# Shared turns with spread routing steps, norms and turned rows written in place, two shared products behind the last expert tile

## The chip, the cores and the metric

The kernel runs on one core of a Trainium2 chip. The metric is the device time of one execution in microseconds; lower is better. The engines of a core are PE (matmul, with its weight loads as PEld), DVE (vector), ACT (scalar, activation tables), POOL (GpSimd) and SP (issues most DMAs). Each has its own queue and takes its instructions in order; they wait for each other by semaphores.

## What is computed

Four residual blocks on `x` of 32 sequences of 256 tokens with 128 columns. The change lies in the first two, retention and a mixture of experts with one expert per token and a shared product:

```python
x = x + _L0_attn_ref(_layernorm(x, axis=-1), ...)
x = x + _L0_ffn_ref(_layernorm(x, axis=-1), ...)

def _L0_ffn_ref(hidden_states, w_router, gate_up_proj, down_proj, w_gate, w_up, w_down):
    x = hidden_states.reshape(-1, h)
    logits = x @ w_router.T
    _, top_idx = jax.lax.top_k(logits, TOP_K)
    mask = jax.nn.one_hot(top_idx, E, dtype=logits.dtype).sum(axis=1)
    scores = jax.nn.sigmoid(logits) * mask
    masked_inputs = scores.T[:, :, None] * x[None, :, :]
    gate_up = jnp.einsum('eth,ehf->etf', masked_inputs, gate_up_proj)
    gate, up = jnp.split(gate_up, 2, axis=-1)
    expert_out = jnp.einsum('etf,efh->eth', up * jax.nn.silu(gate), down_proj)
    shared = jax.nn.silu(x @ w_gate.T) * (x @ w_up.T) @ w_down.T
    out = shared + expert_out.sum(axis=0)
    return out.reshape(b, s, h)
```

Then come an attention over each sequence (the chip time from 423 us on) and a last block on selected rows. They are the same in both kernels.

## The kernel before

`retention_and_experts` is the first program block, up to about 423 us. It has four stages, and each engine's code is written out by hand in the order in which the engine runs it.

**The retention loop.** `pipeline(engine, steps, n, first)` writes, for each turn `it`, the steps in the order of its list; a step with lag k works on sequence `it - k`. The 32 sequences take turns 0 to 31, and the later lags drain in the turns after. For a sequence, DVE takes statistics of the rows (`stats2_of`, `moments2`), POOL turns them into a factor and a shift in four small operations (`inv_std2`), ACT writes the norm (`norm2`, into `h2`, two buffers), PE turns it (`transpose_h2`), ACT copies the turned rows from PSUM (`copy_h2T`, into `h2T`, two buffers), and POOL copies both into buffers for all sequences (`keep_h2` into `h2_all`, `keep_h2T` into `h2T_all`). Every fourth sequence PE multiplies by the router (`route`) and turns the logits (`turn_logits`).

**Shared products and routing.** For each sequence PE does `up(s)` (8 PE instructions in the profile) and `down(s)` (8), ACT the Silu (`gate_of`), DVE the product (`gated`) and the addition to `x` (`add_shared`). `up(s)` waits for the gate and the product of sequence s-2, whose buffers it uses. Beside that DVE finds the expert of each token in two halves of 32 tiles: `choose` (five operations), `span` (a scan), `slots` (row numbers), then `count_tiles` and `find_experts` (four operations of 0.8 us for each half). PE's `count_rows(half)` counts tokens; ACT's `copy_counts` and `score_rows` copy the counts and take the sigmoid. ACT has two activation tables to load for this, Sigmoid and Silu. DVE's `scale_rows(s)` multiplies a sequence's rows by their score, and POOL's `scatter(t)` sends a tile of rows, by an indirect DMA, to their place in DRAM (`sorted_in`): 64 of them. A scatter waits for its rows (`scaled`) and its row numbers (`slot_done`).

**Expert tiles.** SP waits for `expert_done`, for the padding rows and for all 64 scatters, and loads tiles of sorted rows. PE turns them (L1041), multiplies them by their expert's weights (L1050, L1063), 40 pairs of tiles; POOL scatters the results (L517, `y_rows`).

**The end of the block.** SP waits for the last result to be stored (`stored`), starts two loads of results, and all engines meet (L102 to L104) before the attention starts.

In the code before, the shared products begin with `shared_first` at lag 8, one turn for each of the first five; ACT loads the Silu table in `counts_first`; and all operations of `span`, `slots` and `gated` come on DVE after the whole pipeline.

## Time and profile before

| | us |
|---|---|
| median of 3 runs | 1022.21 (1020.53 to 1022.84) |
| profiled execution, device time | 1023.18 |
| its span in the profile | 1021.4 |
| PE busy over the span | 913.6 (89%) |
| DVE, ACT, POOL busy | 716.1, 638.3, 609.7 |
| retention loop, about | 20 to 181 |
| shared products and routing, about | 181 to 290 |
| expert tiles, about | 291 to 411 |
| end of the block, about | 411 to 423 |

The span is the time from the first to the last recorded instruction; the device time has 1.8 us more around it. A busy share is an average over stages with different limits, so the stages are read one by one. In the timelines a row is a run of instructions of one line: its start, its length, engine and line, what is written and read, how many, and in brackets how long the engine sat idle before and who ended it. `banks` is PSUM; `r_v_pad` holds the shared product, `r_qT` the gate, since these buffers are used again; `r_h` is also the small buffer `h2`, and `h` the large one.

### The profile page before, as it was taken

What the parts mean: (1) busy time and instruction counts of PE and PEld (TensorE: products, weight loads), DVE (VectorE), ACT (ScalarE), POOL (GpSimd) and SP (SyncE); (2) the same over time, 40 slices, a digit from 0 to 9 for tenths busy, and PEclk for the clock granted to TensorE, in tenths of its full rate; (3) what the DMA queues carried; (4) which work ended last, traced back from release to release, by engine and by line L of the source; (5) the groups of instructions that cost most, each with busy time, mean ns of one, the idle gap of its engine ahead of it and who ended that gap; (6) DMA issues with size and microseconds to landing.
All of it is one profiled execution on the core that took longest, in us unless ns stands there. A gap on an engine that the chain in (4) does not pass through costs nothing. (4 is left out here: it accounts for less than half of the span.)

```text
span 1021.4 us, 28611 instructions
## 1 busy us (share of the span) xinstructions
PE 913.6 (89%) x10122; PEld 687.7 (67%) x10122; DVE 716.1 (70%) x1564; ACT 638.3 (62%) x1306; POOL 609.7 (60%) x1278
## 2 busy tenths in 40 slices
PE   6999999788989999269999999999999999935776
PEld 5888888677989999145666666666666666524654
DVE  4888898567545444366888888888888888727652
ACT  4777776331224444227888888888888888743552
POOL 4777776566737767554666676766666665334003
PEclk9999999899999999559999999999999999976989
DMA  8200000412123332153353434453444434102000
GB/s 321 116 3 2 3 2 2 135 40 86 51 67 96 96 93 74 56 165 117 118 158 117 140 121 153 132 159 117 137 124 128 137 117 131 42 21 64 4 2 21
DMA packets 68571, 93.71 MB, mean 92 GB/s; under 512 B 11474, under 2 KB 60242, under 8 KB 63954
## 3 DMA queue, kind: packets, MB, share of 16 engines
q1 hardware_dynamic: 63186, 80.76, 25.6%
q0 software_dynamic: 5248, 11.15, 3.1%
q8 instruction: 83, 1.36, 0.6%
q14 instruction: 54, 0.44, 0.1%
HBM read 57.60 MB, written 33.23 MB: 89 GB/s over the span
## 5 line engine op out<-in xcount | busy, mean ns | idle before, releaser
L1461 DVE TENSOR_REDUCE a_neg_max<-a_slot 128x4 f32<-128x1024 f32 x256 | 306.0, 1218 | 79.3 <-PE a_slot L1598 62.1
L1550 ACT ACTIVATE a_pT<-a_slot 128x1024 f32<-128x1024 f32 x256 | 255.5, 1026 | 8.6 <-PE a_slot L1598 5.1
L1631 PE MATMUL a_ps_o<-a_pT,a_v_pad 128*32 128x256 f32 x2048 | 137.9, 387 | 0.0
L1598 PE MATMUL a_slot<-a_k_stack,a_q_stack 62*128 62x256 f32 x1024 | 120.9, 317 | 5.7 <-DMA a_q_stack<-q_dram 3.8
L1598 PE MATMUL a_slot<-a_q_stack,a_k_stack 64*128 64x256 f32 x1024 | 114.6, 312 | 3.6 <-ACT a_pT L1550 1.9
L1598 PEld LDWEIGHTS a_slot<-a_k_stack,a_q_stack 62*128 62x128 f32 x1024 | 79.7, 192 | 48.1 <-issue 22.2
L517 POOL DMA_INDIRECT y_rows<-h,m_token x80 | 81.1, 1014 | 47.0 <-issue 33.0
L1598 PEld LDWEIGHTS a_slot<-a_q_stack,a_k_stack 64*128 64x128 f32 x1024 | 75.5, 187 | 34.8 <-issue 23.4
L560 DVE TENSOR_TENSOR r_score<-banks,r_decay 128x512 f32<-128x512 f32 x128 | 81.3, 677 | 7.0 <-PE banks L917 7.0
L1631 PEld LDWEIGHTS a_ps_o<-a_pT,a_v_pad 128*32 128x32 f32 x2048 | 53.6, 109 | 45.7 <-issue 19.4
L500 POOL DMA_INDIRECT sorted_in<-h,m_slot x64 | 65.3, 1020 | 30.0 <-issue 17.0
L1050 PE MATMUL banks<-r_kT,h 128*128 128x128 f32 x640 | 79.5, 278 | 0.0
L1050 PEld LDWEIGHTS banks<-r_kT,h 128*128 128x128 f32 x640 | 76.1, 195 | 0.0
L745 DVE COPY h<-expert_up 128x512 f32 x80 | 31.3, 433 | 57.4 <-PE banks L1050 56.6
L986 PE MATMUL banks<-h2T,shared_up 128*128 128x256 f32 x256 | 64.6, 399 | 4.3 <-DVE r_v_pad L675 4.3
L758 ACT ACTIVATE r_h<-x,r_shift,r_rstd 128x128 f32<-128x128 f32 x128 | 56.7, 497 | 9.2 <-POOL r_shift L445 8.8
L832 ACT ACTIVATE r_qT<-banks 128x512 f32<-128x512 f32 x32 | 19.1, 597 | 66.3 <-PE banks L986 66.3
L869 ACT ACTIVATE h<-banks 128x512 f32<-128x512 f32 x40 | 23.9, 599 | 57.3 <-PE banks L1050 57.3
L986 PEld LDWEIGHTS banks<-h2T,shared_up 128*128 128x128 f32 x256 | 49.4, 202 | 11.8 <-issue 4.9
L1362 POOL TENSOR_TENSOR a_max_part<-a_neg_max,a_zeros 128x16 fp32r<-128x16 f32 x64 | 13.6, 212 | 71.9 <-DVE a_neg_max L1461 69.6
L1391 POOL TENSOR_TENSOR a_v_pad<-a_v_tok,a_zeros 128x128 f32<-128x128 f32 x64 | 24.2, 399 | 52.4 <-PE a_ps_o L1631 52.4
L1364 POOL TENSOR_TENSOR a_part<-a_qk,a_part 128x256 fp32r<-128x256 f32 x64 | 46.5, 727 | 5.0
(291 smaller groups left out, 2038.0 us busy)
## 6 DMA issues: line engine op xcount, KB each, us to landing
a_k_stack<-k_dram SPq DMA_DIRECT2D x64, 256.0 KB, 3.0
a_q_stack<-q_dram SPq DMA_DIRECT2D x64, 256.0 KB, 3.6
k_dram<-a_part SPq DMA_DIRECT2D x64, 128.0 KB, 2.3
q_dram<-a_part SPq DMA_DIRECT2D x32, 256.0 KB, 2.1
h<-sorted_in SPq DMA_DIRECT2D x80, 66.0 KB, 2.0
expert_up<-in_eu_dram SPq DMA_DIRECT2D x1, 4096.0 KB, 22.7
out_dram<-e_x_plus_h SPq DMA_DIRECT2D x32, 128.0 KB, 2.1
h<-y_rows SPq DMA_DIRECT2D x7, 512.0 KB, 4.3
```

The source lines that it names most:

```text
L500: nc.gpsimd.indirect_dma_start(sorted_in, bass.IndirectOffsetOnAxis(ap=slot[:, t:t + 1], axis=0), h2_all[:, t, :], None).then_inc(scattere ...
L517: nc.gpsimd.indirect_dma_start(y_rows, bass.IndirectOffsetOnAxis(ap=token[:, at:at + 1], axis=0), ye[:, t % RING, j], None).then_inc(store ...
L560: nc.vector.tensor_tensor(score[:, p, tile], ps_score[tile][:], own, ALU.mult).then_inc(score_done, 1)
L745: ins = nc.vector.tensor_copy(w_pair[:, p % 2, j], w_up[:, dve_experts[t][j]])
L758: ins = nc.scalar.activation(h[:, p, t], x_sb[:, s * TPS + t, :], ACT.Identity, bias=shift[:, p, t:t + 1], scale=rstd[:, p, t:t + 1])
L986: ins = nc.tensor.matmul(bank[2 * which + s % 2][:, f * S:(f + 1) * S], shared_up[:, which, f], h2T_all[:, s * S:(s + 1) * S], start=True, ...
L1050: ins = nc.tensor.matmul(bank[PAIR * (p % 2) + j][:, f * P:(f + 1) * P], w_pair[:, p % 2, j, f * P:(f + 1) * P], xeT[:, p % 2, j], start=T ...
L1364: nc.gpsimd.tensor_tensor(low.bitcast(F32R), value, high, ALU.subtract).then_inc(steps, 1)
L1461: nc.vector.tensor_reduce(neg_max[:, p, half, t, :, g], slots[SLOT_OF["m", j]][:].rearrange("p (c r) s -> p c r s", c=TILES), AX.X, ALU.ma ...
L1550: nc.scalar.activation(pT[:, j % PT_RING], slots[SLOT_OF["e", j]][:], ACT.Exp).then_inc(e_read, 1)
L1598: ins = nc.tensor.matmul(slot[:, tile * UT + r], weights[at, n, half, g * UT + r, of_weights].bitcast(F32R), moving[at, n, half, g * UT + ...
L1631: ins = nc.tensor.matmul(ps_o[q * APAD:(q + 1) * APAD, g // 2], v_pad[:, p, t, g * UNIT + q], pT[:, (2 * g + t) % PT_RING, q], start=g % 2 ...
```

## The change

Four things are changed.

1. **Norms and turned rows.** `norm2` writes straight into `h2_all`, `copy_h2T` straight into `h2T_all`. POOL's two copies per sequence are gone, with the waits on them; `scale_rows` now waits for the norm and for its turning.
2. **The drain of the loop.** The first count and `up(0)` stand at lag 3 of the last sequence, `up(1)`, `down(0)`, `up(2)` in the turn after it, and then one `down` and one `up` in each turn. ACT loads the Silu table two turns earlier (`silu_first`). DVE scales the first four sequences inside the loop (`scale_first`) and does the first scan and row numbers ahead of the last sequence's `residual` (`place_first`). POOL sends two tiles ahead of the last `inv_std2`.
3. **Routing of the second half.** DVE's operations of `choose(1, ...)`, `span`, `slots` and `find_experts` are spread over the shared turns 7 to 26, at most one small group for each turn. `LATE_CHOICE` is 7; PE's second count stands in turn 13.
4. **Two sequences later.** With `DEFERRED = 2` the shared products of sequences 30 and 31 come behind the last expert tile, on PE, ACT and DVE.

The core of the diff (renamed parameters, removed semaphores and repeated forms left out):

```diff
-SLOT_STARTS = (0, 8, PART_TILES, PART_TILES + 8)
+SLOT_STARTS = (0, 8, PART_TILES, PART_TILES + 8, PART_TILES + 20)
-LATE_CHOICE = 6
-DRAIN_ROWS = 3
-DRAIN_GATES = 4
-DRAIN_SHARED = 5
+LATE_CHOICE = 7
+DEFERRED = 2
+DRAIN_ROWS = 5
+DRAIN_GATES = 6
+DRAIN_SHARED = 6
...
-            pipeline(pool, [(keep_h2, 6), (inv_std2, 5), (decay_q, 3), (inv_std1, 0), (prepare, 0), (scatter_first, 5), (keep_h2T, 5)],
-                     B, B)
+            pipeline(pool, [(scatter_first(range(0, 2)), 5), (inv_std2, 5), (scatter_first(range(2, DRAIN_ROWS)), 6), 
+                            (decay_q, 3), (inv_std1, 0), (prepare, 0)], B, B)
...
             def scale_rows(s):
-                after(dve, h2_kept, s + 1)
+                after(dve, h2_done, s + 1)
+                after(dve, h2T_done, s + 1)
...
+            def scale_first(s, p, r):
+                if CHOOSE + 5 <= s < CHOOSE + 5 + FIRST_SCALED // 2:
+                    n = 2 * (s - CHOOSE - 5)
+                    if n == 0:
+                        dve.wait_ge(row_score_done, 1)
+                    scale_rows(n)
+                    scale_rows(n + 1)
+
+            def place_first(s, p, r):
+                if s == B - 1:
+                    span(0)
+                    slots(0)
...
+            pipeline(dve, [(stats1_of, 0), (settle2, 5), (decayed_k, 3), (moments2, 5), D_[0], D_[1], (settle1, 0), D_[2],
+                           (mask_state, 3), (moments1, 0), D_[3], (place_first, 4), (residual, 4), (stats2_of, 4), (choose_first, 0),
+                           (scale_first, 0), (gate_first, 4)], B, B)
...
-            for s in range(2, B):
+            for s in range(2, B - DEFERRED):
                 gated(s)
                 add_shared(s - 2)
...
+                if s in range(LATE_CHOICE, LATE_CHOICE + 5):
+                    choose(1, s - LATE_CHOICE)
+                elif s == LATE_CHOICE + 6:
                     span(1)
...
+                elif s in range(LATE_CHOICE + 7, LATE_CHOICE + 10):
+                    slots(s - LATE_CHOICE - 5)
+                elif s == LATE_CHOICE + 10:
                     count_tiles()
...
+                elif s in range(LATE_CHOICE + 11, LATE_CHOICE + 19):
+                    find_experts(s - LATE_CHOICE - 11)
+                elif s == LATE_CHOICE + 19:
+                    number_experts()
...
+            for s in range(B - DEFERRED, B):
+                gated(s)
+                if s > B - DEFERRED:
+                    add_shared(s - 1)
+            add_shared(B - 1)
...
             def copy_h2T(s, p, r):
                 after(act, h2T_done, s + 1)
-                after(act, h2T_kept, s - 1)
-                nc.scalar.copy(h2T[:, p], ps_tail[:, 0:S]).then_inc(h2T_copied, 1)
+                nc.scalar.copy(h2T_all[:, s * S:(s + 1) * S], ps_tail[:, 0:S]).then_inc(h2T_copied, 1)
...
+            pipeline(act, [(copy_qk, 3), (copy_v, 3), (copy_hT, 2), (copy_h2T, 6), (counts_first, 4), (norm1, 1), (keep_logits, 8), (copy_logits, 7),
+                           (copy_oT, 4), (gates_first((0,)), 4), (gates_first((1,)), 5), (gates_first((2, 3)), 6), (gates_first((4,)), 7), (gates_first((5,)), 8),
+                           (norm2, 5), (silu_first, 2), (score_first, 0)], B, B)
...
             def shared_first(s, p, r):
-                if s == B - DRAIN_SHARED:
+                if s == B - 1:
                     pe.wait_ge(tables, 2)
+                    pe.wait_ge(state_done, B)
+                    pe.wait_ge(score_done, RT * B)
                     count_rows(0)
...
+                    up(0)
+
+            def shared_next(n):
+                def step(s, p, r):
+                    if s == B - 1:
+                        if n == 0:
+                            up(1)
+                        down(n)
+                        up(n + 2)
+                return step
...
-                    pe.wait_ge(shared_added, B)
+                    pe.wait_ge(shared_added, B - DEFERRED)
...
+            for s in range(B - DEFERRED, B):
+                up(s)
+                if s == B - DEFERRED + 1:
+                    pe.wait_ge(ye_copied, NX // PAIR)
+                if s > B - DEFERRED:
+                    down(s - 1)
+            down(B - 1)
```

What this does to the order is seen at three places. The first is PE where the loop drains. Before (L932 sums the last sequence's values, L947 is its output, L955 turns norms of the last two sequences, L978 and L979 count, L986 is `up`, L997 `down`):

```order
L947 MATMUL banks<-r_wo,r_oT 128x128 x2
L955 MATMUL banks<-ident,r_h 128x128 x2
L932 MATMUL banks<-r_score,r_v_pad 32x128 x16
L938 MATMUL banks<-r_q_late,r_state 128x128
L972 MATMUL banks<-ident,r_logits_T 128x128 x2
L947 MATMUL banks<-r_wo,r_oT 128x128 x2
L955 MATMUL banks<-ident,r_h 128x128 x2
L978 MATMUL banks<-chosen,m_ones_b 128x512
L979 MATMUL banks<-chosen,m_before_b 128x512
L986 MATMUL banks<-h2T,shared_up 128x256 x4
L955 MATMUL banks<-ident,r_h 128x128 x2
L986 MATMUL banks<-h2T,shared_up 128x256 x8
```

And now, at the same place (L974 turns norms, L996 and L997 count, L1004 is `up`, L951 sums the last values, L1015 is `down`):

```order
L974 MATMUL banks<-ident,h 128x128 x2
L996 MATMUL banks<-chosen,m_ones_b 128x512
L997 MATMUL banks<-chosen,m_before_b 128x512
L1004 MATMUL banks<-h2T,shared_up 128x256 x4
L951 MATMUL banks<-r_score,r_v_pad 32x128 x16
L957 MATMUL banks<-r_q_late,r_state 128x128
L990 MATMUL banks<-ident,r_logits_T 128x128 x2
L966 MATMUL banks<-r_wo,r_oT 128x128 x2
L974 MATMUL banks<-ident,h 128x128 x2
L1004 MATMUL banks<-h2T,shared_up 128x256 x4
L1015 MATMUL banks<-shared_down,r_v_pad 128x128 x4
L1004 MATMUL banks<-h2T,shared_up 128x256 x4
```

The counts and `up(0)` moved ahead of the last sequence's values, and three groups of shared products stand ahead of the last turning of norms, where one stood.

The second place is POOL, at the end of the loop. Before (L464 and L460 are the two copies, L438 to L445 `inv_std2`, L500 the scatters):

```order
L464 COPY h2T<-r_h2T 128x256
L460 COPY h<-r_h 128x2x128
L438 TENSOR_TENSOR r_ve<-r_mv,r_eps 128x2
L440 TENSOR_TENSOR r_minus_mean<-r_zeros,r_mv 128x2
L443 TENSOR_TENSOR r_rstd<-r_ve,r_half 128x2
L445 TENSOR_TENSOR r_shift<-r_minus_mean,r_rstd 128x2
L500 DMA sorted_in<-h,m_slot 135168x132 x3
L464 COPY h2T<-r_h2T 128x256
L460 COPY h<-r_h 128x2x128
```

And now (L487 are the scatters):

```order
L442 TENSOR_TENSOR r_shift<-r_minus_mean,r_rstd 128x2
L487 DMA sorted_in<-h,m_slot 135168x132 x2
L435 TENSOR_TENSOR r_ve<-r_mv,r_eps 128x2
L437 TENSOR_TENSOR r_minus_mean<-r_zeros,r_mv 128x2
L440 TENSOR_TENSOR r_rstd<-r_ve,r_half 128x2
L442 TENSOR_TENSOR r_shift<-r_minus_mean,r_rstd 128x2
L487 DMA sorted_in<-h,m_slot 135168x132 x62
```

The copies are gone, two scatters moved ahead of the last norm's four steps, and 62 scatters follow it in one row.

The third is DVE, in the shared turns. Before (L675 is `gated`, L681 `add_shared`, L618 `scale_rows`, L663 to L667 `find_experts`):

```order
L675 TENSOR_TENSOR r_v_pad<-r_qT,banks 128x512
L681 TENSOR_TENSOR x<-x,banks 128x256
L618 TENSOR_TENSOR h<-h,m_score 128x2x128
L663 TENSOR_TENSOR work<-tile_no,m_end 1x640
L665 TENSOR_REDUCE m_expert_f<-work 1x40
L666 TENSOR_TENSOR work<-work,m_skipped 1x640
L667 TENSOR_REDUCE m_row_f<-work 1x40
L675 TENSOR_TENSOR r_v_pad<-r_qT,banks 128x512
```

And now (L648, L654, L608 and L663 to L670 in their place):

```order
L648 TENSOR_TENSOR r_v_pad<-r_qT,banks 128x512
L654 TENSOR_TENSOR x<-x,banks 128x256
L608 TENSOR_TENSOR h<-h,m_score 128x2x128
L663 TENSOR_TENSOR work<-tile_no,m_end 1x640
L648 TENSOR_TENSOR r_v_pad<-r_qT,banks 128x512
L654 TENSOR_TENSOR x<-x,banks 128x256
L608 TENSOR_TENSOR h<-h,m_score 128x2x128
L666 TENSOR_REDUCE m_expert_f<-work 1x40
```

Four operations stood between two products; now one does.

## Rows read from the trace of the kernel before

**Rows 1.** windows by stage: busy us (instructions) of PE, PEld, DVE, ACT, POOL; then the clock.

```profile
179.00:192.00 13.00, 6.82 (x63) 5.00 (x64) 7.56 (x24) 6.66 (x15) 5.79 (x15) 0.95 0.63 211
...
210.90:231.00 20.10, 16.08 (x85) 14.11 (x86) 13.37 (x31) 5.99 (x9) 10.62 (x10) 0.92 0.11 38
231.00:243.30 12.30, 8.38 (x50) 7.41 (x50) 11.79 (x25) 1.79 (x3) 7.24 (x6) 1.00 0.40 122
243.30:286.00 42.70, 42.70 (x261) 39.33 (x260) 22.39 (x50) 9.55 (x16) 32.58 (x34) 1.00 0.16 52
```

**Rows 2.** the same view, 20 us of the retention loop.

```profile
60.00:80.00 20.00, 20.00 (x281) 16.67 (x281) 17.55 (x58) 15.10 (x44) 16.43 (x52) 1.00 0.01 3
```

**Rows 3.** PE's timeline at the drain: start, us, instructions, idle before.

```profile
183.84 0.71 PE L947 MATMUL banks<-r_wo,r_oT 128*128 128x128 f32 x4 [0.63 <-ACT r_oT L794]
...
185.83 1.89 PE L986 MATMUL banks<-h2T,shared_up 128*128 128x256 f32 x8
191.82 0.69 PE L955 MATMUL banks<-ident,r_h 128*128 128x128 f32 x2 [4.10 <-ACT r_h L758]
192.31 6.21 PE L986 MATMUL banks<-h2T,shared_up 128*128 128x256 f32 x16
```

**Rows 4.** PE's timeline, the second half's counts and a late product.

```profile
214.53 0.57 PE L978 MATMUL banks<-chosen,m_ones_b 128*128 128x512 bf16 x1 [3.66 <-DVE chosen L606]
...
237.56 1.97 PE L986 MATMUL banks<-h2T,shared_up 128*128 128x256 f32 x8 [1.78 <-DVE r_v_pad L675]
```

**Rows 5.** ACT's timeline at the drain.

```profile
175.09 0.35 ACT L780 COPY r_kT<-banks 128x256 f32<-128x256 f32 x1
...
186.42 1.28 ACT L842 ACT_TABLE_LOAD   x1
187.72 0.37 ACT L804 COPY r_h2T<-banks 128x256 f32<-128x256 f32 x1
```

**Rows 6.** DVE's timeline: a norm's last step, a shared product, the second scan.

```profile
185.70 0.25 DVE L580 BATCH_NORM_AGGREGATE r_mv<-r_stats 128x2 f32<-128x6 f32 x2
...
192.28 0.69 DVE L675 TENSOR_TENSOR r_v_pad<-r_qT,banks 128x512 f32<-128x512 f32 x1 [2.16 <-ACT r_qT L832]
...
223.65 1.26 DVE L634 TENSOR_TENSOR_SCAN r_decay<-m_same,m_total 128x528 f32<-128x528 f32 x1
```

**Rows 7.** POOL's timeline: a norm's first step, then scatters of rows.

```profile
189.36 0.29 POOL L438 TENSOR_TENSOR r_ve<-r_mv,r_eps 128x2 f32<-128x2 f32 x1
...
191.57 1.21 POOL L500 DMA_INDIRECT sorted_in<-h,m_slot  x1 [0.71 <-issue]
...
223.79 1.88 POOL L500 DMA_INDIRECT sorted_in<-h,m_slot  x1 [0.41 <-DVE h L618]
...
235.31 1.38 POOL L500 DMA_INDIRECT sorted_in<-h,m_slot  x1 [0.30 <-issue]
...
243.36 0.95 POOL L500 DMA_INDIRECT sorted_in<-h,m_slot  x1 [2.03 <-DVE h L618]
...
285.96 0.96 POOL L500 DMA_INDIRECT sorted_in<-h,m_slot  x1 [0.30 <-issue]
```

**Rows 8.** the DMA queue's own wait ahead of the expert tiles.

```profile
SPq L409 <- DMA sorted_in<-h,m_slot: 47.2, 1, 47.2
```

**Rows 9.** PE's timeline into the expert tiles.

```profile
291.51 0.41 PE L1041 MATMUL banks<-ident,h 128*128 128x128 f32 x2 [1.77 <-DMA h<-sorted_in]
...
292.74 3.28 PE L1050 MATMUL banks<-r_kT,h 128*128 128x128 f32 x16
```

**Rows 10.** the timeline of all engines behind the last expert tile.

```profile
410.99 0.37 ACT L874 COPY h<-banks 128x256 f32<-128x256 f32 x1 [1.44 <-PE banks L1063]
...
414.09 0.96 POOL L517 DMA_INDIRECT y_rows<-h,m_token  x1 [0.30 <-issue]
...
416.40 7.44 SPq L161 DMA_DIRECT2D h<-y_rows  x4
422.92 0.10 POOL L1308 MEMSET a_half_pow<- 128x2 f32 x1 [7.87 <-POOLq L104]
```

142 lines of the change are left out of this document (60 added, 82 removed).

## The prediction

> **What bounds the kernel now.** I read the busy shares by stage first, then the timelines of PE and POOL where PE has gaps, then what the DMA queue waits for. In the retention loop PE is busy for 20.00 of 20 us at full clock [rows 2], so what is taken from POOL or added to DVE and ACT there is worth nothing as long as PE does not wait. From 181 to 291.5 us it is different. PE is busy for 6.82 of 13.00, 16.08 of 20.10 and 8.38 of 12.30 us, and only from 243.3 on for all of its time [rows 1]. The gaps have names: 4.10 us on a norm of ACT [rows 3], 3.66 us on `chosen` of DVE, and waits on a product of DVE, of which one is shown, 1.78 us [rows 4]. After the first two the clock is lower: 16 instructions of `up` take 6.21 us where 8 take 1.89 at full clock [rows 3].
>
> But PE is not alone in this stage. POOL's 64 scatters run without a gap from 243.36 to 285.96 us: 34 of them [rows 1, 7], so 42.60 / 33 = 1.291 us each. The DMA queue waits for the last of them to land [rows 8], and the first turning of sorted rows starts at 291.51, 1.77 us after PE had run out of work [rows 9]: 5.55 us behind the start of the last scatter. So two queues end almost together here, PE at 289.7, POOL's rows at 291.5, and the stage ends with the later of the two. That decides the forecast: PE is freed of gaps and of two sequences, POOL only of the waits between its scatters.
>
> **The copies of POOL.** 64 copies leave POOL in the loop, beside a PE without a gap: 0. The norms written in place cost ACT the same instructions: 0. The four scalings in turns 30 and 31 lie beside the same PE: 0, and if DVE should not fit, at most their own length, about 1.4 us.
>
> **The Silu table, two turns earlier.** The load takes 1.28 us, and the next instruction of ACT starts 1.30 us after its start [rows 5]. Before, it delayed the last norms. Now it stands right ahead of the copy of the last sequence's keys, which starts at 175.09 [rows 5] as soon as ACT is free, and the last scores wait for that copy. PE stalls there: 1.3 us (from 0, if ACT gets that far earlier, to 1.3). The Trainium skill (ScalarE: Activation LUTs, What ACT_TABLE_LOAD costs) gives 1283 ns for the load and 1380 ns for a drain that goes with it. The trace agrees with the load, not with a drain: nothing is idle around it. By the page the stall would be 2.7 us and the forecast 1.4 us longer.
>
> **The drain.** The chain to the first free run of scatters goes through the last sequence's output. It starts at 183.84 [rows 3]. It moves by 1.3 us for the table and by 2.1 us for the two counts and `up(0)`, which now stand ahead of it (1.89 us [rows 3] and a few tenths for the counts): 187.2. From there to the last step of the statistics it was 185.70 - 183.84 = 1.86 us [rows 3, 6]; the first `gated` now stands between, 0.69 us [rows 6]: 189.8, and 0.25 us long. POOL's four steps lasted from 189.36 to 0.71 us ahead of 191.57 [rows 7], 1.5 us: they end at 191.5. POOL has sent its first two tiles meanwhile. With some of that 0.7 us of issue the third scatter starts at about 192.0 (190.5 to 193). Before, the first started at 191.57, and gaps of up to 2.03 us and more stood between those that followed [rows 7].
>
> **POOL to the end of the stage.** From the third to the last scatter there are 61 intervals: 61 x 1.291 = 78.8 us. The spread operations now lie beside scatters that nobody waits out. The scan of the second half made a scatter 1.88 us long instead of 0.95, a `find_experts` operation one of 1.38 us [rows 6, 7]; four scatters lay over those operations. I add 0.9 + 4 x 0.4 = 2.5 us (0, if the padding rows that SP sends in the same stretch were the cause, to 0.9 + 8 x 0.43 = 4.3). Last scatter: 192.0 + 78.8 + 2.5 = 273.3, against 285.96: **12.7 us earlier**, and with the same 5.55 us the expert tiles start at 278.8. Does POOL have to wait for DVE? Row numbers of the second half come in turns 14 to 16. Turn 14 begins on PE at about 224 (189 + 13 x 2.62 + 1), the numbers are there some 5 us later, and the 33rd scatter is due at 192.0 + 30 x 1.291 = 230.7: about 2 us to spare.
>
> The Trainium skill (SBUF — State Buffer, Who interferes with whom) says that DVE's two-input operations get into the way of POOL only where POOL reads, its reductions never, and that what a scatter needs is the writing side. The row of 1.38 us is not what that says. By that rule the 2.5 us fall away and the time is 1007.5.
>
> **PE to the end of the stage.** A turn of the shared products is 16 instructions, and 42.70 us hold 261 [rows 1]: 2.62 us. After the last sequence's output (187.2) PE turns norms and starts `up(1)` at about 189 (1.3 us as from 183.84 to the counts before 185.83 [rows 3], and a gate more on ACT). One operation of DVE for each turn leaves no gap, since a product may be about 2 us late before `up` two turns on waits for it. With 29.3 turns and 1.5 us for route, turning and counts PE has ended sequence 29 at 189 + 76.8 + 1.5 = 267.3. So PE now waits 11.5 us for sorted rows. The 5.2 us of the two deferred sequences would have fitted into that wait: **deferring them gains nothing here**.
>
> **Clock at the entry.** PE enters the tiles after a long idle time. It did so before too: 3.28 us for the first 16 instructions [rows 9]. After 4.10 us of idle the loss was 6.21 - 2 x 1.89 = 2.4 us [rows 3]. I take 0.5 us more than before (0 to 1.5).
>
> **Behind the last tile.** Before, ACT's last copy started at 410.99, POOL's last scatter of results at 414.09, SP's next loads at 416.40 when these were stored, and the next block's first instruction at 422.92 [rows 10]. The deferred work starts with PE at about 410.9: two turns, 5.2 us, and about 1 us for the last product and addition: 417.2. SP with its two loads is there at about 417.4 (estimate, half a microsecond each). Hidden, with 0.2 us to spare: 0 (from 0 to 5.2, if these products run at half clock). Cover: the storing of results. Every wait that this adds stands behind the last tile on PE, ACT and DVE, and only the meeting of all engines is queued behind it.
>
> **The sum.** 12.7 - 0.5 = 12.2 us. Against the profiled execution 1023.18 - 12.2 = 1011.0; it lies 1.0 us above the median of the three runs, and the forecast for a median is 1022.2 - 12.2 = **1010.0**.
>
> **The rivals.**
> - *Nothing slows the scatters* (2.5 us less): 1007.5. For it: 33 intervals of 1.291 us with three operations of DVE per turn beside them [rows 1, 7]. Against it: the rows of 1.38 and 1.88 us.
> - *PE decides.* The tiles would start at about 268, 23 us earlier: about 999. For that the last scatter must start by 262.5, with an interval below (262.5 - 192.0) / 61 = 1.16 us. The steady mean is 1.291.
> - *Rows come late, or the tail shows.* PE's clock falls in the drain, the turns come 3 to 6 us later and POOL waits for row numbers after all; or the deferred products run at half clock: 2 to 6 us less gain, 1012 to 1016.
> - *Slower: POOL's scatters beside a DVE that no longer pauses.* With more than (285.96 - 192.0) / 61 = 1.54 us each the stage ends later than before; at the 1.88 us of the worst row the last starts at 306.7 and the time is about 1043. Against it: the 33 intervals.
> - *No change:* the earlier start of the tiles is given back by a wait in them. Nothing in the trace points to one.
>
> **How the numbers follow.** The forecast (1008.5 to 1012) has 0.48, no slowing of the scatters 0.22, PE decides 0.03, late rows or tail 0.20, no change 0.03, slower 0.04. A measurement of this kernel can tell about 0.2%, 2 us, from no change. So faster is 0.93, same 0.03, slower 0.04. The range takes in the case without slowing and its earlier start (1005.5) and most of the late ones (1015.5).
>
> **What would show it.** POOL: the third scatter near 192, the last near 273, and hardly an idle row between them. PE: no gap over 1 us between 190 and 267, then one of about 11 us, ended by the DMA of sorted rows, and half clock after it. `DVE chosen` no longer among those who are waited for. Behind the tiles the next block starts some 12 us after the last tile's product, as before. The forecast is wrong if PE is still the last at the entry, if POOL's idle time ahead of the scatters is again on DVE, or if the loop's turns are longer than before.

## The result and the profile after

The changed kernel takes 1007.06 us (median of 4 runs, 1006.55 to 1009.74) where the kernel before takes 1022.02. The recorded ratio over all runs is 0.9864 (95% interval 0.9844 to 0.9884); that of the two medians is 0.9854. Run again beside experiments it took 1008.40 us (6 runs, 1005.21 to 1011.72; ratio 0.9878, 0.9855 to 0.9902). The median of all ten runs is 1007.8. The forecast was 1010.0 with a range from 1005.5 to 1015.5. The profiled execution took 1006.87 us, its span 1005.1, which is 16.3 us less than before.

The stages first, in the view of rows 1: stretch, its length, busy us (instructions) of PE, PEld, DVE, ACT and POOL, granted clock, DMA share, GB/s.

```profile
181.00:194.00 13.00, 11.31 (x92) 9.55 (x93) 8.45 (x24) 5.33 (x13) 7.98 (x13) 1.00 0.58 198
194.00:214.10 20.10, 20.10 (x126) 17.78 (x125) 12.40 (x29) 7.83 (x13) 15.22 (x17) 1.00 0.30 80
214.10:243.30 29.20, 29.20 (x180) 26.77 (x180) 24.67 (x60) 7.11 (x13) 22.49 (x23) 1.00 0.25 77
243.30:267.20 23.90, 23.47 (x149) 21.46 (x147) 15.87 (x35) 5.01 (x9) 18.11 (x20) 1.00 0.22 69
267.20:275.50 8.30, 0.00 (x0) 0.00 (x0) 1.91 (x6) 0.00 (x0) 2.82 (x3) 0.67 0.20 58
275.50:296.00 20.50, 20.30 (x162) 19.91 (x163) 8.68 (x25) 7.78 (x19) 8.21 (x8) 0.89 0.31 80
```

PE has lost its gaps between 194 and 267 us: 20.10 of 20.10 and 29.20 of 29.20 us, where it had 16.08 of 20.10 and 8.38 of 12.30 [rows 1]. Nearly all of its waiting now stands in one piece, from 267.2 to 275.5 us, and behind that the granted clock is 0.89 on the mean.

PE's timeline, at the last scores, the drain and the entry into the tiles (start, us, instructions; idle before and who ended it):

```profile
176.67 1.15 PE L936 MATMUL banks<-r_qT,r_kT 32*128 32x256 f32 x16 [1.16 <-ACT r_kT L791]
...
186.30 0.71 PE L966 MATMUL banks<-r_wo,r_oT 128*128 128x128 f32 x4 [0.63 <-ACT r_oT L805]
...
266.02 1.13 PE L1015 MATMUL banks<-shared_down,r_v_pad 128*128 128x128 f32 x8 [0.38 <-DVE x L654]
275.55 0.66 PE L1067 MATMUL banks<-ident,h 128*128 128x128 f32 x2 [8.40 <-DMA h<-sorted_in]
...
276.84 3.55 PE L1076 MATMUL banks<-r_kT,h 128*128 128x128 f32 x16
```

POOL's timeline: the first scatter, the first of the norm's last steps, the third scatter and the last one:

```profile
186.34 1.21 POOL L487 DMA_INDIRECT sorted_in<-h,m_slot  x1 [2.23 <-issue]
...
188.89 0.20 POOL L435 TENSOR_TENSOR r_ve<-r_mv,r_eps 128x2 f32<-128x2 f32 x1
...
190.47 1.03 POOL L487 DMA_INDIRECT sorted_in<-h,m_slot  x1 [0.16 <-issue]
...
269.67 0.96 POOL L487 DMA_INDIRECT sorted_in<-h,m_slot  x1 [0.30 <-issue]
```

The 64 scatters now take 83.33 us from the first start to the last, where they took 94.39 [rows 7], and the first starts 5.23 us earlier. The tiles start 5.88 us behind the last one's start, much as before (5.55) [rows 7, 9]: 275.55 instead of 291.51. So PE, which ended its products at 267.15, waits for POOL's rows. Before, it waited 1.77 us there [rows 9].

Behind the last tile, all engines:

```profile
393.86 1.15 PE L1089 MATMUL banks<-r_score,h 128*128 x8 [0.65 <-DVE h L731]
...
394.85 3.62 PE L1004 MATMUL banks<-h2T,shared_up 128*128 128x256 f32 x16
...
398.30 0.96 POOL L506 DMA_INDIRECT y_rows<-h,m_token  x1 [0.31 <-issue]
...
400.63 7.41 SPq L162 DMA_DIRECT2D h<-y_rows  x4
401.08 0.42 DVE L654 TENSOR_TENSOR x<-x,banks 128x256 f32<-128x256 f32 x1 [0.92 <-PE banks L1015]
407.12 0.10 POOL L1340 MEMSET a_half_pow<- 128x2 f32 x1 [7.86 <-POOLq L105]
```

The two deferred sequences end with DVE's addition at 401.50, 5.6 us ahead of the next block. That block starts at 407.12, as far behind POOL's last scatter as before (8.82 and 8.83 us [rows 10]). So the deferred work is hidden.

Single runs of one kernel differ by 2 to 8 us here, and much of that arises behind this block, in code that no kernel of this study changes: from the block's end to the span's end it was 598.5 us in the kernel before, 598.0 in the changed one, 596.5 in its second profile and 602.9 in the shorter chain without the deferral. There the time goes with the granted clock: the stretch from 300 us behind the block's end to the span's end took 296.5 us at 0.95 in the second profile of the changed kernel, 297.8 at 0.93 in its first, and 302.8 at 0.91 in that experiment. So beside the medians I give three times from each trace, where a few tenths can be told. The wait is PE's idle time just ahead of the tiles. A ratio is taken against runs of the kernel before that stood beside that kernel (their medians are 1021.40 to 1022.02), and it need not be the quotient of two medians.

| kernel | median us | ratio to before (95%) | last scatter starts | PE's wait, tiles start | block ends |
|---|---|---|---|---|---|
| before | 1022.02 | 1 | 285.96 | 1.77, 291.51 | 422.92 |
| changed | 1007.06 | 0.9864 (0.9844 to 0.9884) | 269.67 | 8.40, 275.55 | 407.12 |
| changed, again | 1008.40 | 0.9878 (0.9855 to 0.9902) | 270.21 | 8.18, 275.86 | 406.88 |
| no deferral | 1008.24 | 0.9863 (0.9847 to 0.9880) | 270.10 | 3.08, 275.87 | 407.74 |
| find_experts grouped | 1008.22 | 0.9861 (0.9846 to 0.9876) | 270.69 | 5.82, 276.50 | 408.85 |
| no spread | 1010.92 | 0.9901 (0.9883 to 0.9918) | 275.65 | 2.02, 281.46 | 411.65 |
| before, copies only | 1016.23 | 0.9942 (0.9929 to 0.9956) | 282.39 | 1.22, 288.25 | 417.87 |
| 30 fillers on PE | 1010.85 | 0.9893 (0.9869 to 0.9916) | 270.17 | none, 280.42 | 410.04 |
| 16 fillers on PE | 1006.23 | 0.9849 (0.9833 to 0.9864) | 270.18 | 1.36, 275.89 | 407.58 |
| scaling on ACT | 1006.45 | 0.9855 (0.9831 to 0.9880) | 268.63 | 7.18, 274.41 | 406.53 |
| shorter chain | 1004.50 | 0.9838 (0.9815 to 0.9862) | 267.42 | 7.10, 273.11 | 404.31 |
| shorter chain, no deferral | 1004.14 | 0.9831 (0.9819 to 0.9844) | 267.66 | 2.01, 273.46 | 404.64 |
| shorter chain, 14 fillers | 1006.53 | 0.9849 (0.9834 to 0.9865) | 268.11 | 0.87, 273.60 | 403.72 |
| shorter chain, no deferral, 3 fillers | 1002.50 | 0.9815 (0.9799 to 0.9831) | 267.23 | 0.45, 272.78 | 402.76 |

### The profile page after: what moved, and what is told of

It is laid out like the page before. It is cut to its first block and busy times, and to the rows that moved or that the text cites. A ratio compares the mean times of both kernels' runs of the same rounds, so it can differ in the third digit from the quotient of the medians.

```text
span 1005.1 us, 28514 instructions
## 1 busy us (share of the span) xinstructions
PE 905.1 (90%) x10122; PEld 681.8 (68%) x10122; DVE 715.1 (71%) x1568; ACT 637.3 (63%) x1306; POOL 586.9 (58%) x1214
## 3 DMA queue, kind: packets, MB, share of 16 engines
q8 instruction: 83, 1.36, 0.5%
## 5 line engine op out<-in xcount | busy, mean ns | idle before, releaser
L549 DVE TENSOR_TENSOR r_score<-banks,r_decay 128x512 f32<-128x512 f32 x128 | 81.3, 677 | 6.1 <-PE banks L936 6.0
L487 POOL DMA_INDIRECT sorted_in<-h,m_slot x64 | 63.7, 996 | 21.3 <-issue 19.8
L1004 PE MATMUL banks<-h2T,shared_up 128*128 128x256 f32 x256 | 60.4, 379 | 0.0
L1004 PEld LDWEIGHTS banks<-h2T,shared_up 128*128 128x128 f32 x256 | 46.4, 190 | 5.3
L440 POOL TENSOR_TENSOR r_rstd<-r_ve,r_half 128x2 f32<-128x2 f32 x64 | 45.0, 703 | 5.0
```

Source lines behind the costliest of these rows:

```text
L440: nc.gpsimd.tensor_tensor(rstd[:, p], ve[:], half[:], ALU.pow).then_inc(rstd_done, 1)
L487: nc.gpsimd.indirect_dma_start(sorted_in, bass.IndirectOffsetOnAxis(ap=slot[:, t:t + 1], axis=0), h2_all[:, t, :], None).then_inc(scattere ...
L549: nc.vector.tensor_tensor(score[:, p, tile], ps_score[tile][:], own, ALU.mult).then_inc(score_done, 1)
L1004: ins = nc.tensor.matmul(bank[2 * which + s % 2][:, f * S:(f + 1) * S], shared_up[:, which, f], h2T_all[:, s * S:(s + 1) * S], start=True, ...
```

## Experiments

**Is the deferral worth anything?** The two sequences go back ahead of the tiles.

```diff
-DEFERRED = 2
+DEFERRED = 0
```

> The changed kernel with the two deferred sequences' products put back ahead of the expert tiles. Theory (POOL's scatters set the entry into the tiles, PE idles 8.4 us there): PE ends its products 5.2 us later, at about 272.4 us, its idle time shrinks to about 3 us, the tiles start where they did (275.5 us, within 0.3) and the time is the changed kernel's within 0.5 us, 1006.6 to 1007.6. Rival (PE sets the entry, and the deferral is what the change gains by): the tiles start up to 5.2 us later and the time is about 1012.

PE's timeline at the entry:

```profile
275.87 1.47 PE L1066 MATMUL banks<-ident,h 128*128 128x128 f32 x4 [3.08 <-DMA h<-sorted_in]
```

PE's wait falls from 8.2 to 8.4 us to 3.08, by the 5.2 us of two turns, and the tiles start at 275.87, where they do in the changed kernel's second profile (275.86). The time lies between the changed kernel's two medians, 0.6 us above the range that was expected, and the block ends 0.6 to 0.9 us later, of which 0.3 to 0.85 lies behind the tiles' start, where the first product takes 3.64 us. At the entry the deferral is worth nothing: POOL sets it.

**What does the grouping of find_experts cost?**

```diff
-                elif s in range(LATE_CHOICE + 11, LATE_CHOICE + 19):
-                    find_experts(s - LATE_CHOICE - 11)
+                elif s in (LATE_CHOICE + 11, LATE_CHOICE + 12):
+                    for n in range(4):
+                        find_experts(4 * (s - LATE_CHOICE - 11) + n)
```

> The changed kernel with the eight find_experts operations of DVE again in two turns, four in a row in each, all else as it is. Theory (a scatter that starts while DVE is in an operation with two SBUF inputs waits for nearly its end; spread, one such operation at a time rarely meets the start of a scatter): the grouped ones lengthen about four scatters by 0.3 to 0.4 us each, as they did before the change, and the last scatter starts 1.0 to 1.5 us later: 1008.1 to 1008.6. PE is some 2 us late for these two turns, which its 8.4 us of idle time take up. Rival 1 (the scatters do not mind DVE, the rows of 1.28 and 1.38 us were the padding rows' doing): 1007.1, no change. Rival 2 (PE's lateness counts): 1010 to 1011.

PE's timeline at the second group, and two of POOL's scatters there:

```profile
247.09 1.97 PE L1005 MATMUL banks<-h2T,shared_up 128*128 128x256 f32 x8 [1.79 <-DVE r_v_pad L648]
```

```profile
243.14 1.38 POOL L487 DMA_INDIRECT sorted_in<-h,m_slot  x1 [0.30 <-DVE h L608]
244.83 1.39 POOL L487 DMA_INDIRECT sorted_in<-h,m_slot  x1 [0.30 <-issue]
```

The long scatters are back (a third one takes 1.19 us), and PE is late twice, by 0.66 and 1.79 us, which its idle time takes up (5.82 instead of 8.40). But from the first to the last scatter it is 83.75 us against 83.33 and 83.34: 0.4 us, not 1.0 to 1.5. A scatter that is pushed by one operation misses the scaling that it would have met later, so costs of this kind do not add up. What the scatters are longer than 0.955 us is 1.12 us in all from 236 to 246 us, against 0.35 in the changed kernel, but 0.14 from there to 262 us, against 0.58. In the median nothing is to be told. The block ends 1.7 to 2.0 us later, of which 0.6 to 1.0 is there at the tiles' start; behind it the first product takes 3.62 us and the second 2.42 (the clock, below). The mechanism is there, its price is small.

**What is the spreading of all routing steps worth?** Choice, span, slots and find_experts stand in the turns of before, the rest of the change stays (of the diff only DVE's part; PE's counts and ACT's score and counts move along).

```diff
+                if s == LATE_CHOICE - 1:
+                    for n in range(2):
+                        choose(1, n)
+                elif s == LATE_CHOICE:
+                    for n in range(2, 5):
+                        choose(1, n)
+                elif s == LATE_CHOICE + 2:
+                    span(1)
+                    slots(2)
+                elif s == LATE_CHOICE + 3:
+                    slots(3)
+                    slots(4)
...
+                elif s in (LATE_CHOICE + 5, LATE_CHOICE + 6):
+                    for n in range(4):
+                        find_experts(4 * (s - LATE_CHOICE - 5) + n)
```

> The changed kernel with the routing steps of the second half in the few turns in which they stood before (choice in two turns, span with the first slots, two slots groups in one turn, find_experts in two turns; on DVE, ACT and PE), while the drain, the copies and the deferral stay changed. Theory (spreading takes away about 11 of the 16 us, the waits between the scatters; the earlier first scatters give the other 5): PE waits for the choice again, POOL waits for scaled rows and row numbers, and the last scatter starts 5 to 10 us later than in the changed kernel: 1012 to 1017. Rival (the earlier scaling in turns 2 and 3, which stays, is what ended POOL's waits, and the spreading itself is worth little): at most 2 us, 1007 to 1009.

PE's timeline at the counts and the entry, and two scatters of POOL:

```profile
209.01 0.59 PE L1004 MATMUL banks<-chosen,m_before_b 128*128 128x512 bf16 x1 [4.61 <-DVE chosen L595]
...
281.46 0.41 PE L1074 MATMUL banks<-ident,h 128*128 128x128 f32 x2 [2.02 <-DMA h<-sorted_in]
...
282.98 1.95 PE L1083 MATMUL banks<-r_kT,h 128*128 128x128 f32 x16
```

```profile
226.05 0.96 POOL L487 DMA_INDIRECT sorted_in<-h,m_slot  x1 [1.83 <-DVE h L608]
...
238.30 0.96 POOL L487 DMA_INDIRECT sorted_in<-h,m_slot  x1 [2.03 <-DVE h L608]
```

PE waits for `chosen` again, its turns come late, so DVE scales late, and POOL waits for scaled rows. The last scatter starts 5.4 to 6.0 us later than in the changed kernel. That lies in the 5 to 10 us of the theory. The median is only 2.5 to 3.9 us longer (1010.92, forecast 1012 to 1017): 0.8 to 1.4 us came back between the tiles' start and the block's end (130.19 us against 131.57 and 131.02), where the first product here takes 1.95 us instead of 3.55 and 2.83 (see the clock, below). The block ends 4.5 to 4.8 us later; the rest is within the scatter of the runs behind it.

Two things can be added from this trace. What stays in it is a part of the change that the list ahead of the prediction leaves out: in the turns of sequences 2 and 3 DVE scales two sequences instead of one. POOL's scatters wait for scaled rows in 7 places here and in 9 in the kernel before, for 7.6 instead of 13.0 us; how much of that is the earlier scaling's, no run shows. And the deferral is not worth nothing here. PE waits only 2.02 us for the rows, with two turns of 5.2 us taken out; with them put back it would have been the later one by some 3.2 us (an estimate from these two numbers; it was not run).

**What are the copies worth?** The kernel before with POOL's two copies gone and both results written in place (diff cut to that).

```diff
-            pipeline(pool, [(keep_h2, 6), (inv_std2, 5), (decay_q, 3), (inv_std1, 0), (prepare, 0), (scatter_first, 5), (keep_h2T, 5)],
+            pipeline(pool, [(inv_std2, 5), (decay_q, 3), (inv_std1, 0), (prepare, 0), (scatter_first, 5)],
...
-                norm(s, p, h2, rstd2, shift2, h2_done)
+                norm(s, p, h2_all[:, s * TPS:(s + 1) * TPS, 0:D], rstd2, shift2, h2_done)
...
-                nc.scalar.copy(h2T[:, p], ps_tail[:, 0:S]).then_inc(h2T_copied, 1)
+                nc.scalar.copy(h2T_all[:, s * S:(s + 1) * S], ps_tail[:, 0:S]).then_inc(h2T_copied, 1)
```

> The kernel before with norms and turned rows written straight to their buffers and POOL's copies gone; nothing else changed. Theory of the prediction (the copies are worth nothing in the loop, where PE has no gap): 1022.0 within 0.9. Rival, formed after the trace of the changed kernel: in the drain of the kernel before, POOL's last norm steps stood behind two such copies (188.15 to 189.36 us, which waited for a turned row), though their statistics were there at 185.70; without the copies they start up to 3.4 us earlier, PE's 4.10 us wait for that norm shrinks, and everything behind it moves by 2 to 3.5 us: 1018.5 to 1020.

POOL's timeline at the drain, with the first scatter, then PE's, the rows that answer to the 4.10 and the 6.21 us of rows 3:

```profile
186.15 0.31 POOL L434 TENSOR_TENSOR r_ve<-r_mv,r_eps 128x2 f32<-128x2 f32 x1 [2.60 <-DVE r_mv L566]
...
191.23 1.21 POOL L486 DMA_INDIRECT sorted_in<-h,m_slot  x1 [3.32 <-issue]
```

```profile
189.04 0.44 PE L941 MATMUL banks<-ident,h 128*128 128x128 f32 x2 [1.19 <-ACT h L745]
189.32 3.67 PE L971 MATMUL banks<-h2T,shared_up 128*128 128x256 f32 x16
```

The norm's last steps start at 186.15 instead of 189.36 [rows 7]: two copies stood ahead of them on POOL, the first of which waited for a turned row. PE's wait falls to 1.19 us, and the tiles start 3.3 us earlier. But the gain does not come by POOL's start: the first scatter moves by 0.34 us only (191.57 to 191.23), 0.94 us behind the end of the row numbers on DVE (190.29). It comes along the train of scatters. Two copies that stood between them, from 195.31 to 196.06 us, are gone; and after the shorter wait 16 instructions of `up` take 3.67 us instead of 6.21, so the shared products behind them, and with them DVE's scalings and the second choice, stand 5.5 us earlier (`chosen` begins at 208.25 instead of 213.78). From the first to the last scatter it is 91.16 us instead of 94.39. So the prediction's 0 is refuted. The time falls by 5.6 us, more than the rival gave: 1.8 us of it lie in the tiles (from their start to the block's end 129.62 us against 131.41), again with a first product of 1.95 us; the rest, about half a us, is within the scatter of the runs.

**Does PE's wait cost its clock?** First the changed kernel once more, as a measure, and with it matmuls of no use in PE's wait.

> The changed kernel itself once more, as the measure for the three kernels beside it: 1006.5 to 1008.5 us. The tiles start some 5.9 us behind the last scatter's start, PE waits about 8.4 us for rows, and the first 16 instructions of the first tile take about 3.5 us, as in its first profile; a theory by which the first profile was an odd one would have another wait there.

The wait is as before, 8.18 us, and the block ends at 406.88; the first product took 2.83 us, not about 3.5.

```diff
             pe.wait_ge(down_loaded, 16)
+            for n in range(30):
+                nc.tensor.matmul(bank[6][:, 0:S], shared_up[:, 0, 0], h2T_all[:, 0:S], start=True, stop=True)
```

> The changed kernel with 30 matmuls of no use (some 7.1 us) on PE behind the last shared product ahead of the tiles, into a bank that the first turning overwrites. Theory (PE's wait for rows costs nothing but its clock: in the kernel before, the changed one and the two with 3.08 and 5.82 us of wait the first 16 instructions of the first tile took 3.28 to 3.64 us and the second product started 4.7 to 5.2 us behind the first turning; where the wait was 2.0 or 1.2 us these were 1.95 and 3.1 to 3.5 us): the clock stays up, the tiles start where they did, the second product comes 1.3 to 1.8 us earlier, and the time is 1.3 to 1.8 us below the changed kernel. Rival 1 (the slow first product comes from what else starts there, the loads of rows and weights): no change. Rival 2 (PE sets the entry after all): up to 7 us longer.

PE's timeline with 30 of them, then with 16, and for the 16 two stretches of the windows view, at the first turnings and in the first product:

```profile
267.47 13.12 PE L1063 MATMUL banks<-h2T,shared_up 128*128 128x256 f32 x60
280.42 0.60 PE L1069 MATMUL banks<-ident,h 128*128 128x128 f32 x4
281.27 2.05 PE L1078 MATMUL banks<-r_kT,h 128*128 128x128 f32 x16 [0.24 <-ACT r_kT L879]
```

```profile
267.46 7.07 PE L1063 MATMUL banks<-h2T,shared_up 128*128 128x256 f32 x32
275.89 0.44 PE L1069 MATMUL banks<-ident,h 128*128 128x128 f32 x2 [1.36 <-DMA h<-sorted_in]
276.97 0.44 PE L1069 MATMUL banks<-ident,h 128*128 128x128 f32 x2 [0.63 <-DMA h<-sorted_in]
277.24 2.95 PE L1078 MATMUL banks<-r_kT,h 128*128 128x128 f32 x16
```

```profile
275.88:277.20 1.32, 0.67 (x4) 0.44 (x5) 0.15 (x1) 0.37 (x1) 0.00 (x0) 1.00 0.52 120
...
278.70:280.20 1.50, 1.50 (x9) 1.50 (x9) 0.00 (x0) 0.00 (x0) 0.00 (x0) 0.50 0.20 46
```

My 30 matmuls were 60 instructions and took 13.12 us, not 7.1: in this type each matmul is two instructions. So the tiles started 4.6 to 4.9 us late, and the time is 2.5 to 3.8 us longer. The clock's part shows all the same: the first product takes 2.05 us, and from the tiles' start to the block's end it is 129.62 us, where the changed kernel has 131.57 and 131.02. Not all of that need be the clock, since the rows had been there for some 4.6 us when these tiles started: the first product explains 0.8 to 1.5 of the 1.4 to 2.0 us. 16 of them:

> The changed kernel with 16 of the matmuls of no use instead of 30: one of them took 13.12 us / 30 = 0.44 us, not the 0.24 us that had been taken, so the 30 ran 4.6 us past the arrival of the rows. 16 take 7.0 us and leave PE about 1.2 us of wait. Theory (the wait costs only the clock): the tiles start where they do in the changed kernel, 5.7 to 5.9 us behind the last scatter's start, the second product of a tile comes about 3.0 us behind the first turning, and the time is 1.0 to 1.8 us below the changed kernel's two medians (1007.1 and 1008.4), 1005.5 to 1007.2. Rival (the filler's gain on the clock in the run before was something else): 1007 to 1008.5.

The median, 1006.23 us, is where it was expected, but the profile doesn't show the reason: the first product takes 2.95 us and the block ends at 407.58. The profiled run took 1008.17 us, the others 1005.40 to 1006.87, and the two below 1006 have a mean granted clock of 0.959 where this one and the fourth have 0.955. So the gain of the others may be the clock's, but no trace of them shows it. The fall did not come in the wait: the clock is still 1.00 when PE turns the first rows, and 0.50 from 278.70 to 280.20 us, in the second half of the first product. So waits of 1.36 and 0.63 us stood ahead of a fall here, and waits of 2.02 and 0.83 us, without the spreading, did not.

**Do the scalings lengthen the scatters?** ACT scales sequences 10 to 31 (DVE's part of the diff, which ends its scaling at sequence 9, is left out).

```diff
+                for t in range(s * TPS, (s + 1) * TPS):
+                    ins = nc.scalar.activation(h2_all[:, t, 0:D], h2_all[:, t, 0:D], ACT.Copy, scale=row_score[:, t:t + 1])
+                ins.then_inc(scaled, 1)
...
                 gate_of(s)
+                n = s - DRAIN_GATES + ACT_SCALED
+                if n < B:
+                    scale_rows(n)
```

> The changed kernel with the scaling of sequences 10 to 31 on ACT (two instructions for each, scaled by the row's score) instead of DVE. Theory (a scatter that starts while DVE has an operation with two inputs in SBUF waits for nearly its end; of the 2.6 us by which scatters are longer than 0.955 us about 1.5 us are starts within a scaling, which are also what locks two scatters to each turn of 2.62 us from 240 to 262 us): these scatters become 0.96 us long, the steady interval there falls from 1.31 to 1.26 us, and the last scatter starts 0.5 to 1.6 us earlier with respect to the first; the time follows, 0.5 to 1.6 us below the changed kernel. Rival (the longer ones come from something else, such as ACT or the padding rows): no change, or longer if ACT is as much in the way.

From the first to the last scatter it is 82.23 us against 83.33 and 83.34: 1.1 us less, inside the forecast. What the scatters are longer than 0.955 us falls from 2.6 to 1.5 us, and from 240 to 262 us they follow each other by 1.26 us, but for those that meet one of the operations left. The tiles start at 274.41, 1.1 to 1.5 us earlier. At the block's end only 0.4 to 0.6 us of this is left: the first two products take 3.62 and 2.27 us, with the clock at 0.50 and then 0.79, and from the tiles' start to the block's end it is 132.12 us. (The median moves by 0.6 to 2.0 us, which by itself would decide nothing.) In this trace ACT's scaling (0.68 us) lies beside scatters of 0.96 us: ACT isn't in the way.

**Does each us off POOL's chain count?** To the scaling on ACT come two moves: the Silu table is loaded behind the copies of the last values and of a turned norm, and the first counts stand ahead of `transpose_h2`, with three scatters ahead of the norm's last steps (lists of the steps, cut).

```diff
+            pipeline(pool, [(scatter_first(range(0, 3)), 5), (inv_std2, 5), (scatter_first(range(3, DRAIN_ROWS)), 6), 
...
+            pipeline(act, [(copy_qk, 3), (copy_v, 3), (copy_hT, 2), (counts_first, 4), (copy_h2T, 6), (silu_first, 3), (norm1, 1), (keep_logits, 8), (copy_logits, 7),
...
+                          (transpose_h, 1), (project_kv, 2), (count_first, 3), (transpose_h2, 5), (shared_first, 3)] +
```

> The changed kernel with three edits on POOL's chain: the Silu table is loaded behind the copy of the last values instead of ahead of the copy of the last keys (PE's stall of 1.16 us goes), the counts of the first half stand ahead of the last turning but one, with three scatters instead of two ahead of POOL's last norm steps (0.85 us), and the scaling of sequences 10 to 31 is on ACT (0.5 to 1.6 us). Theory (POOL's chain decides, each us taken from it comes off the time): the first scatter starts about 2 us earlier, the last one about 3 us, and the time is 2.5 to 3.5 us below the changed kernel; PE's wait ahead of the tiles falls to 6 to 7 us. Rival (PE decides, or the end of the drain is bound by the last output and norm, not by table and counts): 0 to 1.2 us.

POOL's timeline, and DVE's scan of the first half:

```profile
181.56 1.60 POOL L441 TENSOR_TENSOR r_rstd<-r_ve,r_half 128x2 f32<-128x2 f32 x1
...
184.86 1.21 POOL L488 DMA_INDIRECT sorted_in<-h,m_slot  x1 [1.41 <-issue]
```

```profile
181.41 1.26 DVE L621 TENSOR_TENSOR_SCAN r_decay<-m_same,m_total 128x528 f32<-128x528 f32 x1
```

The last scatter starts 2.2 to 2.8 us earlier, the block ends 2.6 to 2.8 us earlier, the median is 2.6 to 3.9 us lower. The stall of 1.16 us is gone. The first scatter starts 1.5 to 2.0 us earlier, so the earlier counts gave 0.3 to 0.85 us: the scan now waits for DVE itself, which still has small copies of its own ahead of it until 181.38.

**The deferral and the clock, once more.** The shorter chain without the deferral; with 14 fillers; and without the deferral with 3 fillers.

> The kernel with the shorter chain of POOL, with the two deferred sequences' products put back ahead of the tiles. There PE had 7.1 us of wait, so it now has 1.9 us. Theory (POOL decides, deferring is worth nothing even here): the tiles start where they did, some 5.7 us behind the last scatter's start, and the time is that of the shorter chain (1004.5) or up to 1.8 us less if the short wait keeps PE's clock up. Rival (PE decides now): up to 5.2 us longer, 1006 to 1010.

The tiles start at 273.46, the block ends 0.3 us later than in the shorter chain, the time is 1004.14 us against 1004.50: again the deferral is worth nothing. The clock falls here behind PE's wait of 2.01 us (first product 3.20 us). The profiled run took 1009.28 us, since 602.9 us of it lie behind the block (above).

> The kernel with the shorter chain of POOL and 14 matmuls of no use (6.1 us of its 7.1 us of wait) ahead of the tiles, the deferral as it is. Theory: both gains add up, 1.0 to 1.8 us below the shorter chain's 1004.5, 1002.7 to 1003.5. Rival (they do not, since the first tiles are bound by rows and weights there): 1004.5.

The trace is as the theory has it, first product 1.95 us, block end 403.72, 0.6 us ahead of the shorter chain's. The median is not: 1006.53, with runs from 1002.39 (the profiled one) to 1007.15. The mean granted clock is 0.959 and 0.957 in the two below 1004 us and 0.952 to 0.955 in the three above 1006; where these lost it, no trace shows. The runs leave this one open.

> The kernel with the shorter chain of POOL, without the deferral, and 3 matmuls of no use (1.3 us) ahead of the tiles: 0.6 us of wait is left, so the clock should be up for certain. Theory (the place of the two sequences is worth nothing in itself, useful work ahead of the tiles keeps the clock up as well as useless work): as the kernel with 14 such matmuls and the deferral, 1002.7 to 1003.5. Rival 1 (behind the tiles these products are dearer or cheaper than ahead of them): they differ by over 1 us. Rival 2 (PE ends too late): 1004 to 1006.

PE's timeline at the entry, then four us of it in the windows view, and the same four us of the changed kernel:

```profile
270.87 1.46 PE L1077 MATMUL banks<-h2T,shared_up 128*128 128x256 f32 x6
272.78 0.44 PE L1083 MATMUL banks<-ident,h 128*128 128x128 f32 x2 [0.45 <-DMA h<-sorted_in]
...
274.06 1.95 PE L1092 MATMUL banks<-r_kT,h 128*128 128x128 f32 x16
```

```profile
272.70:276.70 4.00, 3.35 (x28) 3.11 (x29) 1.48 (x6) 1.40 (x4) 0.00 (x0) 1.00 0.48 110
```

```profile
275.50:279.50 4.00, 3.79 (x17) 3.41 (x18) 0.10 (x1) 0.74 (x2) 0.00 (x0) 0.50 0.49 110
```

In the same time PE has 28 instructions at a granted clock of 1.00, and 17 at 0.50, the lower of its two levels, beside the same traffic (DMA share 0.48 and 0.49, 110 GB/s), so that the loads of rows and weights do not explain the slow product. The block ends at 402.76, 4.1 to 4.4 us ahead of the changed kernel's, and the time is 1002.50 us, ratio 0.9815 (0.9799 to 0.9831): the lowest median of this study. All its runs lie below all runs of the changed kernel; of the shorter chain's runs, with and without the deferral, some are as fast, but in the traces their block ends 1.6 to 1.9 us later.

By the medians rival 1 has its difference: 1002.50 against 1006.53 us of the kernel with 14 fillers and the deferral. In the two traces it is not there: 129.98 and 130.12 us from the tiles' start to the block's end, and 1003.09 and 1002.39 us for the two profiled runs. So in the block the place of the two sequences makes no difference of its own; why the medians differ stays open.

## Why the prediction was right, and where its steps were off

**The frame held.** PE's products and POOL's rows were weighed as two queues that end together, and the later one decides: POOL. PE ended at 267.15 (forecast 267.3), had no gap over 1 us between 190 and 267, and then waited, 8.40 us instead of 11.5, as the rows came sooner. That PE's end was hit so closely is in part luck: `up(1)` began at 187.86 instead of 189, and the turns took 1.0 us more than counted. `DVE chosen` no longer ends anyone's wait. That deferring gains nothing was said, and two runs showed it; without the spreading it would have counted (above).

**The copies: 3.3 us through the drain.** The step "64 copies leave POOL in the loop, beside a PE without a gap: 0" costed only the loop. The two copies in the drain held the last norm on POOL from 185.95 to 189.36 us [rows 6, 7], and so PE, and behind PE's wait its clock. The sum takes POOL's chain of the changed kernel as it will stand, without copies, and is not wrong by this; but the reader is told the wrong owner. The 16 us of the tiles' start divide, by the traces, into 3.3 us for the copies (291.51 to 288.25), 6.8 us for the drain, the earlier scaling and the deferral together (to 281.46), and 5.6 to 5.9 us for the spreading (to 275.55 and 275.86). No run parts the 6.8 us; the traces show the first scatter 4.6 us earlier (191.23 to 186.66) and 2.2 us less from the first to the last (91.16 to 88.99). In another order the shares would differ: the turned row for which POOL's copy waited stood on ACT behind the table load [rows 5], which the new drain moves as well.

**The Silu table.** A stall of 1.16 us, forecast 1.3. The load starts at 174.16 and the copy behind it at 175.46, so no drain shows here either. With the drain that the Trainium skill gives (ScalarE: Activation LUTs, What ACT_TABLE_LOAD costs) it would have been about 2.7 us, an estimate from its two figures; the row decides.

**The third scatter: forecast 192.0, at 190.47** (190.5 to 191.1 in the other profiles with the same drain). The last output came 0.9 us sooner (186.30 instead of 187.2), the statistics and POOL's four steps took 0.3 us less than counted, and the scatter follows them by 0.16 us, not 0.5. Together 1.5 us, in the other profiles 0.9 to 1.5.

**The term that was mis-sized: how much slower the scatters get.** 61 intervals took 79.20 us, not 78.8 + 2.5 = 81.3. The sum took a mean of 1.291 us from a stretch that already held contention, and added contention to it. Where DVE has only one addition left, from 267.15 to 269.67 us in the changed kernel, the interval is 1.26 us. 61 of these are 76.9, so contention in all is 2.3 us, of which the mean already held 1.9. Together with the third scatter this makes the last one start 3.6 us sooner, at 269.67 instead of 273.3. The tiles start 3.3 us sooner (275.55 instead of 278.8), since they follow the last scatter by 5.88 us, not 5.55.

**The rivals.** The time is that of "nothing slows the scatters" (1007.5), but that is luck: the scaling on ACT shows that they are slowed, and its own sum started from the third scatter at 192.0, which was late. "PE decides", "late rows", "slower" and "no change" did not come: the scatters' waits for DVE are 1.5 us in all, in five places, each of about 0.30 us, which is no longer than the pause between any two.

**The clock** was to cost 0.5 us more than before. From the tiles' start to the block's end it is 131.57 and 131.02 us, before 131.41: nothing more. The prediction had read the 3.28 us of before, but not that the kernel before had lost something there which could be had back: 1.3 us against a first product of 1.95 at full clock, 1.8 us over all the tiles (131.41 against 129.62). **The tail** is hidden, as said: from the last product of a tile to the next block 13.26 us, before 13.12. The margin was put at 0.2 us; the deferred work ends 5.6 us ahead of the next block.

The sum was 12.2 us; the spans differ by 16.3, the medians by 15.0 at first and 13.4 in the second measurement. The range holds both times; the narrower one of the likeliest case (1008.5 to 1012) ends just above them.

## What to carry to other kernels

Where two engines end almost together, work out both ends and count only what shortens the later one: here moving 5.2 us of matmuls off the earlier one was worth nothing, and what came off POOL's chain came off the tiles' start. A mean interval taken from a running stretch holds its contention already; take the unobstructed one and add the collisions. And a wait of a matmul engine that costs nothing by itself may cost its clock. Useful work placed in it did as well as work moved out of it, and with three matmuls of no use beside it gave the lowest median; alone, with 2.01 us of wait left, it did not keep the clock up.

## What the runs showed of the hardware

**A scatter that starts inside certain operations of DVE waits for nearly their end.** DVE's timeline of the changed kernel, a reduction, a comparison of two buffers in SBUF and a scaling, then the scatter that starts in each:

```profile
215.95 0.68 DVE L593 TENSOR_REDUCE first<-work 128x32 f32<-128x512 f32 x1
...
218.57 0.69 DVE L595 TENSOR_TENSOR chosen<-rank,first 128x512 bf16<-128x512 f32 x1
...
242.24 0.42 DVE L608 TENSOR_TENSOR h<-h,m_score 128x256 f32<-128x256 f32 x1
```

```profile
216.34 0.96 POOL L487 DMA_INDIRECT sorted_in<-h,m_slot  x1 [0.30 <-DVE h L608]
...
218.86 1.22 POOL L487 DMA_INDIRECT sorted_in<-h,m_slot  x1 [0.31 <-DVE h L608]
...
242.44 1.05 POOL L487 DMA_INDIRECT sorted_in<-h,m_slot  x1 [0.30 <-issue]
```

The scatter at 216.34 starts 0.29 us ahead of the end of a reduction and takes 0.96 us. Those at 218.86 and 242.44 start 0.40 and 0.22 us ahead of the end of an operation with two inputs in SBUF and take 0.26 and 0.09 us longer. So does the one of 1.88 us, which started 0.14 us after the scan [rows 6, 7]: the scan had 1.12 us to go, the scatter was 0.93 longer. In each it went on some 0.1 to 0.2 us ahead of the end. Scatters that started in a shared product, with one input in PSUM, took 0.96 us (209.81 in one from 209.41, 217.60 in one from 217.29), and operations that began after the scatter cost it nothing: the changed kernel's second scan starts at 224.42 in the middle of one that takes 0.96 us. (The first scatter of a train takes 1.21 us even when it starts with DVE idle, as at 186.34, so that not every long one is DVE's doing.) POOL's own arithmetic is longer in a scan too: 1.60 us instead of 0.72 in the shorter chain, above. That the one that issues first goes ahead is what the Trainium skill says (SBUF — State Buffer, Who interferes with whom); here only POOL is seen to wait, since the second scan takes 1.26 us both in the middle of a scatter and, before, ahead of one [rows 6]. That page also infers that a `tensor_tensor` of two SBUF inputs leaves descriptor generation alone; these rows, scatters with 0.09 to 0.26 us of wait in such an operation, say otherwise.

**PE's clock at the entry.** With waits of 0.45 to 1.22 us for the first rows the first product took 1.95 us (copies only, and the two kernels of the shorter chain with fillers), with waits of 3.08 us and more it took 2.83 to 3.64. Between them it went either way: 1.95 us after 2.02 us of wait without the spreading, 2.95 after 1.36 with 16 fillers, 3.20 after 2.01 in the shorter chain without the deferral, 3.28 after 1.77 before [rows 9]. After the long waits the first turnings already run at 0.50 (275.50 to 279.50, above); after the 1.36 us the clock fell only later, in the middle of the first product. What decides stays open.
